# Attention projections in three full blocks, odd heads moved by DMA, and the queues of one batch put into a new order

## The reference, cut to what matters

```python
h = c + gqa(rmsnorm(c, attn_norm_w))            # c: output of the conditional FFN, one of 8 experts per batch
q = (n @ wq.T).reshape(B, S, 16, 16)            # n = rmsnorm(c) * attn_norm_w
k = (n @ wk.T).reshape(B, S, 4, 16)             # each key head serves four query heads
v = (n @ wv.T).reshape(B, S, 4, 16)
attn = softmax(where(causal, q @ k.T / 4, -inf))
out = (attn @ v) @ wo.T
```

## Time and profile before

| | |
|---|---|
| median of 3 runs | 2267.49 us (2262.47 to 2271.82) |
| the profiled execution | 2255.25 us, of which the span is 2253.6 us |
| mean granted clock of TensorE | 0.968 |
| busy share of the span | PE 92%, PEld 79%, DVE 61%, ACT 49%, POOL 43% |
| PE busy in 430 to 1040 us | 591.71 of 610 us |

### The profile page before, as it was taken

How to read it: one execution, slowest core, us unless ns; L and a number is a source line. 1 busy time by engine, 2 the same in 40 slices (tenths; PEclk the granted TensorE clock), 3 DMA queues, 4 the chain that set the end, 5 groups by cost and what they waited for, 6 DMA issues and landing times. The chain is left out here.

```text
span 2253.6 us, 50867 instructions
## 1 busy us (share of the span) xinstructions
PE 2084.0 (92%) x16744; PEld 1776.2 (79%) x16776; DVE 1372.2 (61%) x2834; ACT 1114.2 (49%) x2206; POOL 971.9 (43%) x1062
## 2 busy tenths in 40 slices
PE   6999978999999999997996999999849999999997
PEld 5999976666666666664996999999738888888886
DVE  5888854567666666676563777777554445444442
ACT  5666643455555555554563333333224545545442
POOL 0000011245545455454664545545135565655653
PEclk9999997999999999998998999999969999999998
DMA  6666630222212222122995444444224545445442
GB/s 231 238 238 238 239 123 25 100 69 67 85 60 87 73 72 82 63 77 78 313 305 180 152 147 149 156 147 153 98 68 111 115 88 114 93 110 113 89 87 31
DMA packets 127209, 285.06 MB, mean 126 GB/s; under 512 B 20705, under 2 KB 58338, under 8 KB 120674
## 3 DMA queue, kind: packets, MB, share of 16 engines
q1 hardware_dynamic: 77026, 173.04, 23.0%
q0 software_dynamic: 50048, 110.14, 19.2%
HBM read 187.17 MB, written 95.42 MB: 125 GB/s over the span
## 5 line engine op out<-in xcount | busy, mean ns | idle before, releaser
L1043 DVE TENSOR_REDUCE neg_max<-ring 128x2 f32<-128x512 f32 (+1 forms) x384 | 251.2, 681 | 111.0 <-remote 87.7
L814 POOL TENSOR_SCALAR_AFFINE_SELECT weights_diag<-weights_diag 128x512 f32<-128x512 f32 x256 | 155.9, 634 | 320.9 <-ACT weights_diag L926 320.0
L2586 POOL DMA_INDIRECT out<-eo,row_put x128 | 201.3, 1573 | 162.9 <-ACT eo L2651 138.2
L2726 DVE TENSOR_TENSOR ex_hid<-ex_up_ps,gelu 128x512 f32<-128x512 f32 x128 | 87.0, 689 | 173.5 <-ACT gelu L2635 173.5
L2576 POOL DMA_INDIRECT toks<-hs,row_get x128 | 134.8, 1053 | 132.9 <-DVE row_get L2692 97.1
L2635 ACT ACTIVATE gelu<-ex_gate_ps 128x512 f32<-128x512 f32 x128 | 76.3, 596 | 188.4 <-PE ex_up_ps L61 188.4
L2020 POOL DMA_INDIRECT picked_rows<-results,lo_row_now x128 | 144.5, 1129 | 56.4 <-issue 29.3
L926 ACT ACTIVATE weights_diag<-ring 128x512 f32<-128x512 f32 x256 | 138.5, 600 | 34.2 <-PE ring L1570 34.2
L311 POOL DMA_DIRECT2D c<-c_sb x31 | 17.0, 549 | 302.3 <-DVE c_sb L377 302.3
L59 PE MATMUL ex_down_ps<-ex_dn_lo,ex_hid_hi 128*128 128x256 f32 x512 | 144.2, 282 | 2.8 <-issue 2.8
L61 PE MATMUL ex_down_ps<-ex_dn_hi,ex_hid_hi 128*128 128x256 f32 x512 | 143.8, 281 | 0.0
(11 more groups left out here) (368 smaller groups left out, 7662.6 us busy)
## 6 DMA issues: line engine op xcount, KB each, us to landing
ug_raw<-in_w_ug SPq DMA_DIRECT2D x32, 1028.0 KB, 5.1
dn_raw<-in_w_dn SPq DMA_DIRECT2D x32, 640.0 KB, 6.1
q_t<-sorted_rows SPq DMA_DIRECT2D x136, 128.0 KB, 3.2
expert_gu<-in_expert_gu SPq DMA_DIRECT2D x16, 1024.0 KB, 4.8
results<-c0n POOLq DMA_DIRECT2D x33, 256.0 KB
x_raw<-in_x_t SPq DMA_DIRECT2D x32, 256.0 KB, 5.1
c0n<-c SPq DMA_DIRECT2D x32, 256.0 KB, 3.9
c0r<-c SPq DMA_DIRECT2D x32, 256.0 KB
```

The lines of the kernel that those rows point to most:

```text
L814: nc.gpsimd.affine_select(part, part, [[0, G], [1, P]], ALU.is_ge, 0.0, base=0, channel_multiplier=-1).then_inc(kept_done, 1)
L1043: nc.vector.tensor_reduce(out, src, AX_X, ALU.max, negate=True).then_inc(max_done, 1)
L2586: nc.gpsimd.indirect_dma_start(out=out_rows, out_offset=bass.IndirectOffsetOnAxis(ap=at, axis=0), in_=eo[c][:, n, :], in_offset=None, comp ...
```

## The change

The query weights are laid out anew. wq of two neighbouring heads of a group now fills 32 full rows, so that two blocks of queries (one A piece, "q") give all four heads: the even head in rows 0 to 15 of each 32, the odd one in rows 16 to 31. wk and wv share a third block, keys in rows 0 to 15, values in rows 16 to 31. ACT copies that block to kv_t (take_kv); DVE makes k_t from it, with the one now in row 16 (keep_k); PE transposes kv_t (turn_v, two transposes) and DVE takes the values from that (keep_v). The odd heads lie in the wrong rows: four transfers on SP (move_odd_heads) bring them from rows 16 to 31 to rows 0 to 15. The shift goes to row 16 of each 32. The masks are multiplied into the bank ahead of the scores, and each score product covers 128 keys in place of 256. The orders of PE, DVE, ACT and POOL in a body are written anew.

```diff
-        A_ORDER = (("out_proj", -2, B), ("values_q1", -1, B), ("heads_q0", -1, B), ("heads_q1", -1, B), ("q_a", 2, B), ("q_b", 2, B), ("values_q0", 0, B))
-        B_ORDER = (("shift_q0", 0, B), ("norm_t", 2, B), ("h_t", -2, B), ("kv", 2, B), ("route", -2, B + 1), ("shift_q1", 1, B), ("out_t", -1, B))
+        A_ORDER = (("out_proj", -2, B), ("values_q1", -1, B), ("heads_q0", -1, B), ("heads_q1", -1, B), ("q", 2, B), ("values_q0", 0, B))
+        B_ORDER = (("shift_q0", 0, B), ("norm_t", 2, B), ("h_t", -2, B), ("kv", 2, B), ("v_t", 2, B), ("route", -2, B + 1), ("shift_q1", 1, B), ("out_t", -1, B))
...
             def move_shift(b, q):
                 sp.wait_ge(b_free, per_b(f"shift_q{q}", later(b, -q)) + 1)
-                sp.dma_start(q_t[b[1] % 4][0:P:32, :, q * P:(q + 1) * P], shift[q][:]).then_inc(shift_in[q], 16)
+                sp.dma_start(q_t[b[1] % 4][HD:P:32, :, q * P:(q + 1) * P], shift[q][:]).then_inc(shift_in[q], 16)
+
+            def move_odd_heads(i):
+                n = (i[1] + 2) % 4
+                sp.wait_ge(a_free, per_a("q", i) + 1)
+                for g in range(NKV):
+                    sp.dma_start(q_t[n][32 * g:32 * g + HD, 1:G:2, :], q_t[n][32 * g + HD:32 * g + HALF, 0:G:2, :]).then_inc(odd_heads_in, 16)
...
                     load_to_normalise(later(i, 4))
+                if exists(later(i, 2)):
+                    move_odd_heads(i)
                 if exists(later(i, 1)):
                     move_shift(later(i, 1), 1)
...
             def keep_q(i):
-                act.wait_ge(queries_done, times(2, i, 6))
-                nc.scalar.activation(q_t[(i[1] + 2) % 4][:, 2:4, :], piece_a[:].rearrange("p (j s) -> p j s", j=2), ACT.Copy).then_inc(a_free, 1)
+                act.wait_ge(queries_done, times(1, i, 3))
+                nc.scalar.activation(q_t[(i[1] + 2) % 4][:, 0:G:2, :], piece_a[:].rearrange("p (j s) -> p j s", j=2), ACT.Copy).then_inc(a_free, 1)
+
+            def take_kv(i):
+                act.wait_ge(kv_done, times(1, i, 3))
+                until(act, k_t_done, times(1, i, 2))
+                until(act, v_t_done, times(1, i, 2))
+                nc.scalar.activation(kv_t[:], piece_b[:, 0:S], ACT.Copy).then_inc(b_free, 1)
...
+            def masks(i, r):
...
+                for g in range(NKV):
+                    out = slot(2 * r + 1, g)[:].rearrange("p (c s) -> p c s", s=keys)[:, :, q * P:(q + 1) * P]
+                    nc.tensor.matmul(out, at.identb[:], at.maskb[:, 0:512 // keys, :], start=True, stop=False)
...
             def scores(i, r):
...
-                    for g in range(NKV):
-                        rows = slice(32 * g, 32 * g + 32)
-                        nc.tensor.matmul(slot(2 * r + 1, g)[:, c * keys:(c + 1) * keys], q_t[n][rows, j, q * P:(q + 1) * P], k_t[n][rows, 0:keys],
-                                         start=(c == 0), stop=False)
...
+                    for k in range(q + 1):
+                        whole = c == len(heads_) - 1 and k == q
+                        for g in range(NKV):
+                            rows = slice(32 * g, 32 * g + HD)
+                            last = nc.tensor.matmul(slot(2 * r + 1, g)[:, c * keys + k * P:c * keys + (k + 1) * P], q_t[n][rows, j, q * P:(q + 1) * P],
+                                                    k_t[n][rows, k * P:(k + 1) * P], start=False, stop=whole)
...
             def keys_values(i):
...
-                for t in range(TT):
-                    toks = slice(t * P, (t + 1) * P)
-                    c = S + t * 2 * VW
-                    beside(piece_b[:, c:c + 2 * VW], VW, (nt_hi, nt_lo), toks, at.wv, True)
-                    last = beside_last(piece_b[:, c:c + 2 * VW], VW, (nt_hi, nt_lo), toks, at.wv)
-                last.then_inc(kv_done, 1)
+            def turn_v(i):
+                take_b("v_t", i)
                 for t in range(TT):
+                    last = nc.tensor.transpose(piece_b[:, t * P:(t + 1) * P], kv_t[:, t * P:(t + 1) * P], at.ident[:])
+                last.then_inc(v_t_done, 1)
```

More of the change, by code:

```diff
@@ L829, in body @@
             def body(i):
-                if exists(i):
-                    keep_earlier(i, 1)
-                if exists(later(i, -5)):
-                    scatter(later(i, -5), 0)
+                has, scatters = exists(i), exists(later(i, -5))
+                if has:
+                    keep_earlier(i, 1, (0,))
+                if scatters:
+                    scatter(later(i, -5), 0, (0,))
+                if has:
+                    keep_earlier(i, 1, (1,))
+                if even(i) and exists(later(i, -4)):
+                    roots2(later(i, -4))
+                if scatters:
+                    scatter(later(i, -5), 0, (1,))
+                if has:
+                    keep_earlier(i, 1, (2,))
+                if scatters:
+                    scatter(later(i, -5), 1, (0,))
+                if has:
+                    keep_earlier(i, 1, (3,))
+                    keep_earlier(i, 0, (0,))
                 if exists(later(i, 3)):
                     roots(later(i, 3))
-                if even(i) and exists(later(i, -4)):
-                    roots2(later(i, -4))
-                if exists(i):
-                    keep_earlier(i, 0)
-                if exists(later(i, -5)):
-                    scatter(later(i, -5), 1)
+                if has:
+                    keep_earlier(i, 0, (1, 2, 3))
                 if exists(later(i, -2)):
                     add_x(later(i, -2))
+                if scatters:
+                    scatter(later(i, -5), 1, (1,))
             nc.gpsimd.memset(zeros[:], 0.0).then_inc(zeros_set, 1)
@@ L973, in body @@
                 if has:
-                    exps(i, 1, (2, 3))
-                if has_h:
-                    square_sums2(i, later(i, -2))
-                if has:
-                    exps(i, 2, (0, 1))
+                    exps(i, 1, (2,))
                 if even(i) and exists(later(i, -4)):
@@ L981, in body @@
                 if has:
-                    exps(i, 2, (2, 3))
+                    exps(i, 1, (3,))
+                if has_next:
+                    take_kv(i)
+                if has:
+                    exps(i, 2, (0, 1))
+                if exists(later(i, 3)):
+                    normalise(later(i, 3))
+                if has:
+                    exps(i, 2, (2,))
                 if exists(later(i, 1)):
                     keep_shift(i)
+                if has:
+                    exps(i, 2, (3,))
                 if has_next:
                     keep_q(i)
-                if exists(later(i, 3)):
-                    normalise(later(i, 3))
                 if has_before:
@@ L1435, in _ @@
             nc.vector.memset(done_of[:], 0.0).then_inc(ones_done, 1)
-            dve.wait_ge(ones_done, 4)
-            for g in range(NKV):
-                nc.vector.memset(one_rows[32 * g:32 * g + 1, :], 1.0).then_inc(ones_done, 1)
-            dve.wait_ge(ones_done, 4 + NKV)
+            dve.wait_ge(ones_done, 3)
             dve.wait_ge(set_done, 9)
@@ L1703, in body @@
                 if has_scores:
+                    masks(i, 0)
                     scores(i, 0)
+                if has_before:
+                    values(i, 1)
                 if has_next:
                     turn_norm(i)
-                if has_before:
-                    values(i, 1)
                 if has:
                     turned_scores(i, 1)
+                if has_before:
+                    heads(i, 0)
                 if has_h:
                     turn_h(i)
-                if has_before:
-                    heads(i, 0)
                 if has_scores:
+                    masks(i, 1)
                     scores(i, 1)
+                if has_next:
+                    keys_values(i)
                 if has_before:
@@ L1728, in body @@
                 if has_next:
-                    queries(i, "q_b", (2, 3))
+                    queries(i)
                 if has_scores:
                     turn_max(i, 1)
+                    masks(i, 2)
                     scores(i, 2)
```

173 lines of the change are left out of this document (84 added, 89 removed).

## The result

The changed kernel takes 2366.39 us (median; 2361.39 to 2381.88) against 2268.1 us before: ratio 1.0444, 95% interval 1.0398 to 1.0490. It is slower by about 100 us, where 30 us less were predicted, and outside the range. The profiled execution has a span of 2367.3 us (before 2253.6).

A forecast was written before the change was run, and what follows sets the result against it. TensorE was taken to bound each batch: products -1.98, kv_t +0.2 and the odd-heads wait +1.0 gave, with the loop head, 20.85 us against 21.87, together -30 us, so 2238 us; 8-in-10 range 2206 to 2285.

The forecast's parts named there:

- PE is the bound inside a batch: Attention phase: PE busy 591.7 of 610 us with only short waits, so work taken off it comes off the time.
- Products on PE, -1.98 us: PE per batch: queries -1.49, values -0.84, transposes of kv_t +0.25, smaller score products +0.1; 19.5 us in place of 21.5.
- the wait for kv_t: Transposes of keys and values wait for ACT's copy: +0.2 us a batch, between 0 and 0.5.
- This gains nothing and costs nothing: DVE's key and value copies get shorter and its query copy goes; with 196 of 610 us free, no effect on time.
- A new wait in the middle of the batch: Sign of a wrong forecast: a mid-batch wait, for DVE's maxima or kv_t, longer than the one at the batch's end.
- Odd heads, a wait of 1.0 us: Batch end: four SP copies delay the shift to 4.7 us after turn_max against 3.78; PE loses 1.0 us with restart.
- The price of a wait: End wait counted at its length, 1.0 us with restart; no clock fall, since idle 1.45 and 1.59 us left it alone.
- Eaten up: Rival, 2260 us: issues of 0.58 each, shift landing 0.3 later, a wait of 1.9, -7 us; chance 0.19.
- The clock falls: Rival, 2290 us: waits of about 1.7 us halve PE's clock in a third of the batches, +22 us; chance 0.19.
- if all pay, +90: Within the clock rival: if PE's clock falls after the wait in all batches, the kernel is 90 us slower.
- No wait: Rival, 2208 us: the shift lands in time, 19.9 us a batch, -59 us; chance 0.14.
- The sum: Whole batch: 21.5 - 1.98 + 0.2 + 1.0 = 20.7, with the loop head 20.85 us against 21.87.

The follow-up runs named there:

- k_by_act: Changed kernel with k_t made from kv_t by ScalarE in place of DVE's pass; 2341.5 us, ratio 1.0404 to the kernel before.
- best: Changed kernel with shift issued first, odd heads in one copy of 112 partitions, k_t by ScalarE, all batches written out; 2210.3 us, ratio 0.9809.
- both: Changed kernel with the shift issued ahead of the odd heads and k_t made by ScalarE; 2231.7 us, ratio 0.9906 to the kernel before.
- shift_first: Changed kernel with only SP's order altered, the shift issued ahead of the four odd-head copies; 2291.2 us, ratio 1.0167 to the kernel before.
- before_copies: Kernel before, its products unchanged, with four copies within SBUF added on SP ahead of the shift; 2337.0 us, ratio 1.0391.

## Why the prediction was wrong, step by step

*PE is the bound inside a batch*: right for the kernel before. It is what made every new wait count in full.

*Products on PE, -1.98 us.* Near. The batch without the two waits and without a loop is 19.96 us against 21.40 for the kernel before written out: -1.44, where my sum with kv_t says -1.78. The queries' and values' blocks went as priced. The missing 0.3 us are small pieces: the transposes of kv_t take 0.37 for my 0.25, the wait for kv_t 0.29 for 0.2 (from the start of heads_q1 to the next block, 0.64 where it was 0.35), and blocks of transposes in which nothing was changed some 0.05 each more (turn_out 0.58 for 0.53).

*"This gains nothing and costs nothing" for the copies on DVE.* This step failed. I looked at how much DVE was free in the phase, which says nothing of a pass that cannot run beside POOL. The operand moved from PSUM to SBUF, and the pass went from 0.48 to 2.47 us; PE waits 1.2 us for what is queued behind it. The condition that the Trainium skill names (SBUF — State Buffer, "SBUF: two separate sides") stands in this diff: two SBUF inputs, one of them kv_t. A new wait in the middle of the batch stood among my signs of being wrong, for the maxima or for kv_t; it came for v.

*Odd heads, a wait of 1.0 us.* The mechanism was right and each term too small, above all the issues: 4 x 0.42 = 1.7 against 2.74. Even my upper bound of 4 x 0.58 was passed. No row of before had a copy within SBUF, and I took the value by the loads because the rule on engines in the Trainium skill (DMA: Bandwidth & Descriptors, "Why a DMA increments its semaphore by 16 and not by 1") made me put 16 partitions with wide transfers. That section is on engines and semaphores, and I read an issue time into it. The landing took 1.79 for 1.4. The sum was 6.22 for 4.7, which against 3.78 is 2.4 us of wait: k_by_act shows 2.55, the changed kernel, with PE slowed, 2.1.

*The price of a wait.* My sum took a wait at its own length (1.0 us with the restart) and kept the clock for a rival, since all idle times up to 1.59 us had left it alone. This step failed too: the clock fell after 1.24 us, it fell in every batch, and of the 4.5 us that the two waits cost, 1.9 are products at half clock.

*The rivals.* "Eaten up" had the issues at 0.58 each and was the nearest in mechanism; it lacked the second wait. "The clock falls" had the right sign, and part of the mechanism: the clock did fall in every batch. Its "if all pay, +90" comes near the measured loss of 98, but by luck: it holds one wait of 1.75 us and 3.4 us for each fall, where there are two waits, of 3.3 us in sum, and a fall costs 1.6. "No wait" (2208) is near the 2210 us of best, and that is luck as well: by the ratios it is 0.974 against 0.981, and the loop is gone in best.

*The sum.* 20.85 us a batch was forecast, 25.34 came: +4.5. Taking away the two waits gives 4.53 back, but 0.75 of that was in my forecast, which is 20.10 without the end wait. So 3.8 of the 4.5 us are the two waits and the clock that falls with them. The other 0.7 are in both as well (20.81 for 20.10): 0.25 within the batch (19.97 written out, for 21.5 - 1.98 + 0.2 = 19.72) and 0.46 at the loop heads (0.84 for 0.38).

## What to carry to other kernels

Where a diff moves an operand between PSUM and SBUF, look what runs on GpSimd beside it: a short VectorE pass with two SBUF inputs took five times as long here, with VectorE idle for over a third of the phase. Count DMA issues in series, not bytes, between a late producer and a transfer that PE waits for: put the urgent one first on its queue, or fold several copies into one, even if it carries data that nobody needs. Undo two waits together before judging either, since each can hide behind the other. Where TensorE is the bound, price a new wait by its length and by the clock that may fall behind it: here the clock took 1.9 us a batch beside 2.6 us of idle time. And where the clock falls in some batches only, compare single batches with the same instructions: they show its price without a further run.

## What was not expected of the hardware

- Copies within SBUF take 0.62 us each to issue on SyncE (16 partitions), 0.80 (15 partitions, half the bytes), 0.68 (112 partitions), against 0.45 or less for loads.
- PE's clock fell in every batch of the changed kernel, after idle times from 1.2 us on. With one wait of 1.2 us a batch it fell in some batches and not in others (shift_first, 16 of 27), with one of 1.7 us or more in 9 of 27 (before_copies). A fall costs 1.6 us in a batch that is otherwise the same.
- A VectorE pass with two SBUF inputs ended 0.28 to 0.29 us after the end of GpSimd's addition in 27 batches of 27, and took 0.48 us in the five with GpSimd idle.
- A loop over four batches costs some 7 us in one kernel and 18 us in the other.
